# A graph attention layer on one core: PE's order of work in the first group of the preparation

## The reference

```python
h0 = maximum(layernorm(x), 0)              # rows of 256, eps 1e-5
h  = h0 @ W1 + b1
e  = leaky_relu((h @ a1)[:, None] + (h @ a2)[None, :] + b2, 0.2)
att = softmax(where(adj > 0, e, -1e12), axis=1)
out = x + elu(att @ h)
```

## Time and profile before

| | |
|---|---|
| median of three runs | 427.93 us |
| span of the profiled execution, first to last instruction | 422.2 us |
| PE busy | 416.1 us, 99% |
| DVE busy | 374.3 us, 89% |
| ACT busy | 309.0 us, 73% |
| first matmul of the stream that goes on to the main loop (L640 of group 1) | 13.93 us |

### The profile page before, as it was taken

How to read it: one execution, slowest core, us unless ns; L and a number is a source line. 1 busy time by engine, 2 the same in 40 slices (tenths; PEclk the granted TensorE clock), 3 DMA queues, 4 the chain that set the end, 5 groups by cost and what they waited for, 6 DMA issues and landing times.

```text
span 422.2 us, 8433 instructions
## 1 busy us (share of the span) xinstructions
PE 416.1 (99%) x3325; PEld 409.9 (97%) x3325; DVE 374.3 (89%) x404; ACT 309.0 (73%) x306; POOL 24.9 (6%) x44
## 2 busy tenths in 40 slices
PE   8999999999999999999999999999999999999996
PEld 7888899999999999999999999999999999999996
DVE  4897999999998499999995699999992999999955
ACT  4689898999983778867664879768574789586622
POOL 1021100000000400000000400000001200000003
PEclk9999999999999999999999999999999999999999
DMA  8950068555557446648388066657477166566302
GB/s 268 392 214 0 2 212 339 199 200 199 199 200 255 145 166 233 206 147 297 112 308 302 25 205 241 248 146 258 148 260 284 71 231 207 193 224 260 114 3 98
DMA packets 22585, 82.40 MB, mean 195 GB/s; under 512 B 1531, under 2 KB 14113, under 8 KB 14242
## 3 DMA queue, kind: packets, MB, share of 16 engines
q1 hardware_dynamic: 22276, 81.81, 54.8%
q10 hardware_dynamic: 286, 0.27, 0.2%
HBM read 77.86 MB, written 4.21 MB: 194 GB/s over the span
## 4 chain that ended last, share of the span: by engine, by line
PE 96%; DVE 2%; DMA 1%; ACT 0%; issue 0%; ACTq 0%; DVEq 0%
PE ps L771 53%; PE ps L773 27%; PE ps L652 5%; PE ps L793 2%; PE ps L794 2%; PE ps L795 2%; PE ps L640 2%; DMA v_rows<-vectors 1%; DVE adj_s L879 1%; DVE h_raw L864 0%; PE ps L595 0%; PE ps L605 0%; DVE y L1086 0%; PE ps L747 0%; PE ps L621 0%; PE ps L612 0%
## 5 line engine op out<-in xcount | busy, mean ns | idle before, releaser
L773 PE MATMUL ps<-hp_lo,w_hi 128*128 (+1 forms) x936 | 226.8, 282 | 0.0
L771 PE MATMUL ps<-hp_hi,w_hi 128*128 (+1 forms) x936 | 226.8, 282 | 0.0
L879 DVE SCALAR_TENSOR_TENSOR adj_s<-R,p,adj_s 128x1024 f32<-128x1024 f32 x128 | 165.2, 1330 | 24.2 <-ACT adj_s L450 24.0
L771 PEld LDWEIGHTS ps<-hp_hi,w_hi 128*128 128x128 f32 x936 | 176.8, 189 | 0.0
L773 PEld LDWEIGHTS ps<-hp_lo,w_hi 128*128 128x128 f32 x936 | 176.7, 189 | 0.0
L458 ACT ACTIVATE w_hi<-adj_s 128x2048 fp32r<-128x2048 f32 x64 | 122.4, 1912 | 37.5 <-DVE adj_s L879 37.2
L889 DVE SCALAR_TENSOR_TENSOR w_lo<-adj_s,w_hi 128x2048 fp32r<-128x2048 f32 x64 | 145.9, 2280 | 0.0
L450 ACT ACTIVATE adj_s<-adj_s 128x2048 f32<-128x2048 int32 x64 | 122.3, 1910 | 25.9 <-DMA adj_s<-adj_t 25.8
L771 PE MATMUL ps<-hp_hi,w_lo 128*128 (+1 forms) x944 | 123.0, 283 | 0.0
L771 PEld LDWEIGHTS ps<-hp_hi,w_lo 128*128 128x128 f32 x944 | 117.3, 189 | 0.0
L652 PE MATMUL ps<-W1x,hnT 128*128 128x258 f32 x128 | 30.2, 382 | 0.0
(11 more groups left out here) (110 smaller groups left out, 188.6 us busy)
## 6 DMA issues: line engine op xcount, KB each, us to landing
adj_s<-adj_t SPq DMA_DIRECT2D x64, 1024.0 KB, 4.9
x_s<-x SPq DMA_DIRECT2D x7, 512.0 KB, 8.8
o_s<-x SPq DMA_DIRECT2D x3, 1024.0 KB, 7.6
out<-o_s SPq DMA_DIRECT2D x6, 512.0 KB, 6.8
R<-r_rows SPq DMA_DIRECT2D x1, 1536.0 KB, 6.4
adj_s<-x SPq DMA_DIRECT2D x1, 1024.0 KB, 5.5
out<-adj_s SPq DMA_DIRECT2D x8, 128.0 KB, 1.7
x_s<-x SPq DMA_DIRECT2D x2, 256.0 KB, 3.8
```

What stands on the lines that cost most here:

```text
L771: last = pe.matmul(acc, block_w, hh, start=fresh, stop=False)
L773: pe.matmul(acc, block_w, hl, start=False, stop=False)
L879: last = dve.scalar_tensor_tensor(sgn, R[:, ds(ic * CW, CW)], p[:, ds(source(r, c) + s, 1)], sgn, ALU.max, ALU.mult)
```

## The change

PE's and ACT's written orders change for the first group. `WARM` goes from (6, 2, 1) to (9, 2, 3). On PE, `turn_W1` comes directly behind `turn_vectors`, and `weigh` ahead of `transposes(0)`; `spread_b1` comes behind `transposes(0)`, and `weigh_b1` behind `project(0, 0)`. On ACT, `keep_WT` comes ahead of `root(0)`, `keep_wv` ahead of `relu_T(0)`, and `keep_b1` behind it. `weigh` waits for three of the kept columns' counts, no longer for the repeated bias; `weigh_b1` waits for that itself.

```diff
-WARM = (6, 2, 1)
+WARM = (9, 2, 3)
@@ ACT @@
             keep_acol()
             repeat_b1()
+            keep_WT()
             act.wait_ge(eps_ready, 1)
             root(0)
+            normalise(0)
+            keep_wv()
+            relu_T(0)
             keep_b1()
-            normalise(0)
-            keep_WT()
-            relu_T(0)
             root(1)
-            keep_wv()
             keep_ba()
             normalise(1)
@@ PE, weigh @@
-                pe.wait_ge(acol_kept, 4)
+                pe.wait_ge(acol_kept, 3)
@@ PE, weigh_b1 @@
+                pe.wait_ge(acol_kept, 4)
                 pe.wait_ge(hn_ready, KC)
@@ PE @@
             keep_warm(WARM[0])
             pe.wait_ge(pool_c, 3)
             turn_vectors()
-            spread_b1()
+            turn_W1()
             keep_warm(WARM[1])
-            turn_W1()
+            weigh()
             keep_warm(WARM[2])
             transposes(0)
-            weigh()
-            weigh_b1()
+            spread_b1()
             pe.wait_ge(w1x_ready, 1)
             project(0, 0)
+            weigh_b1()
             transposes(1)
```

## The result

The changed kernel took 424.63 us (median of 22 runs, 424.43 to 424.93); the kernel before, run beside it, 427.66 us (22 runs, 423.81 to 429.23). The ratio of the two is 0.9949, 95% interval 0.9929 to 0.9969. (It stands near the quotient of the means, 424.66 to 426.73, and not at that of the medians, 0.993.) The kernel became 0.5% faster where I had forecast 428.7 us, and 424.63 lies outside my range.

A forecast was written before the change was run, and what follows sets the result against it. PE was taken to bound the kernel, so the start of `transposes(1)` decides: 14.67 against 13.93 us, plus 0.05 for a standstill, is 0.79 later. Added to the median of 427.93 this gave 428.7 us, range 427.9 to 429.9.

The forecast's parts named there:

- The step that failed: End of the sum: runs' median 427.93 us, 5.7 above the profiled span of 422.2, plus 0.79 gives 428.7.
- my sum: Chain of starts up to `transposes(1)`: 14.67 us, 0.74 later than before; with 0.05 for a standstill, 0.79 late.
- a second step: TensorE at full clock from around `weigh`'s start, forecast at 6.89 us, with 0.06 added for a slightly late rise.
- My second rival: Clock falls back in the new 1.3 us standstill ahead of `transposes(1)`, costing 2.7 us: 431.4 us; chance 0.03.
- W1 turned: L612's four transposes on PE, moved early, start at 5.12 us and end at 6.18 instead of 8.26.
- PE's idle: PE, free at 13.36 us, stands still for 1.3 us ahead of `transposes(1)`, waiting for `normalise(1)` on ACT.
- The first rival: Clock rises no sooner than about 10.4 us, so `transposes(0)` starts at 9.87; costs 1.5 us: 430.2; chance 0.08.
- The rival that the lag would be swallowed: Lag absorbed between 40 and 50 us, where DVE, ACT and PE hand over to each other: 428.0 us; chance 0.08.
- the rival that `keep_ba` doesn't decide: ACT reaches `normalise(1)` without waiting; `transposes(1)` starts at 13.36, 0.57 us earlier: 427.4 us; chance 0.05.

The follow-up runs named there:

- the first experiment: The kernel before, run again with no edit: median 427.28 us (12 runs, 423.99 to 428.54).
- the first experiments: The first four experiments, beside which the unchanged kernel before ran 35 further times: 17 short runs up to 425.0 us, the others long.
- the last execution: The kernel before, unchanged, third of three further single looks: 427.88 us, span 426.1, clock rising only near 18.8 us.

## Why the prediction was wrong

**The step that failed** is the sentence: "the runs' median of 427.93 stands 5.7 above it for what lies around the program, and I add 0.79 to that." Around the program lie 1.7 to 1.9 us. The profile and the median were of different kinds of executions, and I added a difference worked out for the short kind to a median of the long kind. On the base that belongs to the profile, 422.2 + 1.8 = 424.0, my sum gives 424.8; 424.63 was measured, and 424.74 in the execution that was profiled.

**Behind it stands a second step**, "I take the clock as risen around `weigh`'s start", with the rise of before as if it were one number, 10.4. It isn't: 9.9, 10.4, 10.5, 18.8, and about 4.2 with a fall at 7.6, in five executions of the same kernel. I weighed what holes mean for the rise in the new kernel, and never what they do in the old one from run to run. My second rival even named a fall of the clock, its price of 2.7 us near what the falls cost (3.2 us, 427.2 against 424.0), but I put it in the changed kernel, behind the 1.24 us hole ahead of `transposes(1)`, and gave 0.03. The changed kernel's own profile shows no fall there, and the experiment with a hole ahead of the first transposes has none behind the same 1.24 us either. But in the one with the first hole reopened the clock does fall there, at 17.8: what the rival described can happen. And falls were happening in the kernel before, by the clock in six of the 12 runs of the first experiment, while three more had the late rise's time and clock. That in the changed kernel the rise neither comes late nor is lost again is read from its 22 runs, which lie within 0.5 us, and from one profile; it wins 3.0 us in the median, net of what is lost in the chain.

**Inside the span the steps were right.** By order of the sum: L600 5.12 (4.98 forecast; six passes took 1.28, but the first behind them took longer to start), W1 turned by 6.4 (6.2), `root(0)` 6.90 (6.74), `weigh` 1.02 us long (0.98), `transposes(0)` 8.79 (8.68), `project(0, 0)` 10.89 (10.67), `keep_ba` 13.55 behind 2.35 us of idle (over 2 us), `transposes(1)` 14.75 (14.67), PE's idle 1.24 (1.3), span + 0.8 (+ 0.79). The starts are 0.1 to 0.2 late, and that the ends met within 0.1 is partly luck: `project(0, 0)` was 0.22 late, and the way from there to `transposes(1)`, forecast at 4.00 us, took 3.86. The clock, too, had risen 0.7 us before I took it as risen. Nor is 0.8 the distance between the kernels' ordinary runs: the eight short runs of the kernel before have a median of 424.42, 0.2 under the changed kernel, and the 17 short ones beside the first experiments 424.08, 0.6 under it. The rival that the lag would be swallowed falls by the 403.8 us and by the run with `keep_ba` behind; so does the rival that `keep_ba` doesn't decide, since moving it won 1.3 us. The first rival, a rise no sooner than 10.4, falls for the profiled execution, where it came at 6.2.

On the Trainium skill's rule in TensorE: Matmul & The Clock Gate, "Part 4: PE-mode transpose", the runs show that transposes do run at the full level once it is there (L612's four take 0.60 us in the first experiment's profile and 1.06 in the earlier trace rows). Whether they help to bring it about no run sets apart: fillers or other matmuls stand beside them in front of every rise. The same page, in "Part 1: The HAM clock gate (the "warmup" mystery)", says that the number of slow matmuls at a kernel's start varies from run to run. The traces agree: in the kernel before the first rise came at about 4.2, at 9.9, 10.4, 10.5 and 18.8 us. That sentence was the one to weigh; I had not used it.

What stays open: why some starts of the kernel before rise near 4.2, others near 10 and others at 18.8, and what exactly makes the clock fall. No run here set it apart, and I only know that the same code does all three. Standstills stand in front of every fall, but not every such standstill is followed by one.

## What to carry to other kernels

Before adding anything to a median, take the span of the profiled execution and of timed runs from the same source, and be suspicious where "the rest" is larger than in a sister kernel: the profile may be of another kind than the median. Where PE starts from rest, a prediction needs the whole distribution of runs: small holes among the first matmuls cost little by themselves, but with them came falls of the clock that cost up to some 3 us afterwards. Fill a hole for the pace at which it will be filled (it grows when the clock is up), don't forget that fillers at half pace can hold up the real work (twelve passes held the first transposes until 11.95 us), and look what else an engine holds in order behind a moved wait: `keep_ba` in front of `normalise(1)` gave away 1.3 of the 4.0 us (427.32 to 423.29) that the best order wins in the median.

## What the runs showed of the hardware

An early rise of the clock that is lost again was worse than a later rise that stays: in the first experiment the kernel before took 427.2 to 427.4 us with the first and 424.0 with neither fall nor late rise, and with next to no early fillers it took 424.09 where six gave 427.21.

The profiles hold six falls, in five executions. The standstills of PE between the rise and the fall were 0.96 (in part) and 0.51 us; 0.24 and 1.11; 0.69 (in part) and 0.45; 1.24; 0.19, 0.45, 0.71 and 0.39; and, with eight first fillers, 0.43 and 0.45. Some falls came while PE was at work, one of them (fillers from 7.16, fall at 7.6) over 1 us behind the last standstill. Against this, the changed kernel's profiled execution has 0.33, 0.39 and 1.24 us of standstill at the full level and no fall. Once down, the clock took between some 3 and 10 us to come back, although PE was busy nearly throughout (9.21 of 10.00 us, and 10.00 of 10.00).

And the granted clock in a table of stretches can't be trusted ahead of the first recorded change: in the last execution's stretch from 7.7 to 17.7 us it reads 1.00, while the eight transposes of L640 take 1.97 us. That is why every first rise in this document is read from the pace:

```profile
7.70:17.70 10.00, 9.93 (x39) 1.00 1.09 373
```
